# The delta layer's sixteen heads written out in a row in place of a loop over pairs of heads

## The reference, cut to what matters

```python
xn = _layernorm(x)
x = x + _L0_attn_ref(xn, ...) + _L0_ffn_ref(xn, ...)   # 16 heads; shared and routed experts
xn = _layernorm(x)
x = x + _L1_attn_ref(xn, ...) + _L1_ffn_ref(xn, ...)   # the delta layer; up, relu squared, down
```

```python
state = state * d_t
delta = (v_t - k_t @ state) * b_t
state = state + outer(k_t, delta)
o     = q_t @ state
```

## Time and profile before

| what | value |
| --- | --- |
| runs | 1971.49, 1990.26, 1990.32 us |
| profiled execution | 1971.39 us, span 1969.4 us |
| instructions counted as busy | 35372 |
| TensorE busy | 1749.0 us, 89% of the span |
| VectorE busy | 1519.3 us, 77% |
| ScalarE busy | 1226.4 us, 62% |
| GpSimd busy | 636.4 us, 32% |
| mean granted TensorE clock | 0.971 of full speed |
| data DMAs | 73.55 MB, 11.7% of 16 engines |
| instruction DMAs | 153 packets, 2.11 MB |

### The profile page before, as it was taken

How to read it: one execution, slowest core, us unless ns; L and a number is a source line. 1 busy time by engine, 2 the same in 40 slices (tenths; PEclk the granted TensorE clock), 3 DMA queues, 4 the chain that set the end, 5 groups by cost and what they waited for, 6 DMA issues and landing times.

```text
span 1969.4 us, 35372 instructions
## 1 busy us (share of the span) xinstructions
PE 1749.0 (89%) x12824; PEld 1303.0 (66%) x12824; DVE 1519.3 (77%) x2421; ACT 1226.4 (62%) x2155; POOL 636.4 (32%) x442
## 2 busy tenths in 40 slices
PE   7899999999899778889888889888988888988976
PEld 5667676767657566667766667666776666756665
DVE  8788888888674787887777878778777787877853
ACT  3253534444355567777677877768767786777862
POOL 2212222231230535336053261432605326144140
PEclk9999999999999899999999999999999999999988
DMA  3011110101032001101101011010110101101000
GB/s 131 32 62 38 54 61 31 61 31 62 3 99 65 17 16 39 33 23 33 56 23 33 23 34 55 23 34 23 33 55 23 33 23 34 55 23 33 7 1 22
DMA packets 51465, 75.66 MB, mean 38 GB/s; under 512 B 3392, under 2 KB 41792, under 8 KB 51184
## 3 DMA queue, kind: packets, MB, share of 16 engines
q1 hardware_dynamic: 51312, 73.55, 11.7%
HBM read 72.29 MB, written 1.25 MB: 37 GB/s over the span
## 4 chain that ended last, share of the span: by engine, by line
PE 39%; DVE 12%; ACT 10%; issue 9%; POOL 2%; ACTq 0%; DVEq 0%; POOLq 0%
PE bank L897 6%; PE bank L731 6%; PE bank L852 5%; PE bank L742 4%; DVE d_sil L1311 4%; PE bank L790 2%; DVE d_Rb L1377 2%; PE bank L800 2%; PE bank L764 2%; POOL d_dec L1629 2%; DVE d_W L1385 2%; PE bank L873 1%; PE bank L875 1%; PE bank L874 1%; ACT d_TT L1149 1%
## 5 line engine op out<-in xcount | busy, mean ns | idle before, releaser
L1311 DVE SCALAR_TENSOR_TENSOR d_sil<-d_pre,d_w,d_sil 128x1024 f32<-128x1024 f32 x192 | 298.1, 1553 | 5.9 <-ACT d_pre L1081 5.6
L1635 POOL TENSOR_TENSOR d_Rb<-d_V,d_ones 128x512 bf16<-128x512 f32 x32 | 48.0, 1511 | 711.0 <-ACT d_V L1110 711.0
L1363 DVE CAST_PREDICATED d_X<-tables_sb,bank 128x512 bf16<-128x512 int32 x192 | 134.3, 700 | 147.6 <-PE bank L790 146.9
L731 PE MATMUL bank<-xnT,d_w 128*128 128x512 f32 x480 | 244.1, 644 | 0.8
L189 PE MATMUL bank<-xnT,a_w 128*128 128x512 f32 x512 | 237.0, 597 | 0.0
L1145 ACT ACTIVATE d_T<-bank 128x512 bf16<-128x512 f32 x160 | 98.5, 616 | 107.4 <-PE bank L800 105.1
L1629 POOL TENSOR_TENSOR d_dec<-d_dec,d_qk 128x384 f32<-128x384 f32 x128 | 133.2, 1064 | 44.2 <-DVE d_N L1344 44.2
L852 PEld LDWEIGHTS bank<-d_W,d_N 128*128 128x128 f32 x1024 | 122.7, 193 | 35.0 <-DVE d_W L1385 22.4
L189 PEld LDWEIGHTS bank<-xnT,a_w 128*128 128x128 f32 x512 | 90.9, 192 | 78.5 <-issue 78.5
L731 PEld LDWEIGHTS bank<-xnT,d_w 128*128 128x128 f32 x480 | 89.2, 202 | 79.3 <-issue 79.3
L489 POOL TENSOR_TENSOR a_hidc<-a_hid,a_comb 128x512 f32<-128x512 f32 x32 | 44.4, 1387 | 295.0 <-DVE a_hid L336 295.0
(11 more groups left out here) (211 smaller groups left out, 4497.9 us busy)
## 6 DMA issues: line engine op xcount, KB each, us to landing
d_dec<-decay_scratch SPq DMA_DIRECT2D x32, 512.0 KB, 5.7
a_w<-w SPq DMA_DIRECT2D x16, 897.0 KB, 4.6
d_w<-w SPq DMA_DIRECT2D x16, 776.0 KB, 4.8
a_comb<-comb_scratch SPq DMA_DIRECT2D x16, 512.0 KB, 5.5
d_dec<-decay_scratch SPq DMA_DIRECT2D x32, 256.0 KB, 6.0
d_wo<-w SPq DMA_DIRECT2D x16, 256.0 KB, 3.0
f_w<-w SPq DMA_DIRECT2D x8, 256.0 KB, 3.7
tables_sb<-tables SPq DMA_DIRECT2D x1, 1056.0 KB, 8.4
```

The costliest lines, as they stand in the source:

```text
L731: last = pe.matmul(psum[bank][:, :], cols(slot, (c * KT + k) * P, P), xnT[:, k, h * HALF:(h + 1) * HALF], start=(k == 0), stop=(k == KT - 1))
L1311: dve.scalar_tensor_tensor(sil[c][:, :, :], pre[c % 2][:, :, tap:tap + S], cols(slot, OC + 4 * c + tap, 1), sil[c][:, :, :], ALU.mult, ALU ...
L1363: dve.copy_predicated(left(Xp[lv][:, v], lv), mask.unsqueeze(1).broadcast_to([P, 8, 64]).rearrange("p n (g w) -> p n g w", w=lv), psum[4 + ...
```

## The change

In `layer1_phase` the helper `loop` becomes a Python loop that calls the body for each head with integers. The order of the instructions within every engine's stream, the buffers and the semaphores' counts stay as they are. The hardware loop is gone from all five engines in this layer, with its counter, its jump, and the registers that held counts and addresses. The code of the layer becomes longer: heads 2 to 13 now stand twelve times in each stream where two heads stood before.

```diff
         def loop(engine, body, begun=0):
 
-            if not begun:
-                body(0, 0, 0)
-            body(0, 1, 1)
-            with engine.Fori(1, HEADS // 2 - 1) as j:
-                for slot in range(2):
-                    body(j, slot, j * 2 + slot)
-            body(HEADS // 2 - 1, 0, LAST - 1)
-            body(HEADS // 2 - 1, 1, LAST)
+            for i in range(begun, HEADS):
+                body(i // 2, i % 2, i)
```

## The result

The changed kernel takes 1958.04 us (median of four runs, 1953.93 to 1960.94); the kernel before, with a fourth run, 1987.11 us (1971.49 to 1990.32). The two medians alone give a ratio of 0.985; the recorded comparison of the runs gives 0.9886, with a 95% interval of 0.9845 to 0.9926: faster by 1.1%, clear of the noise and less than 2%. The forecast was 1957.4. The profiled execution took 1959.84 us with a span of 1957.8, against 1971.39 and 1969.4, so 11.6 us of span are to be accounted for; the rest of the difference of medians is the spread of the kernel before, to which the last experiments come.

What follows compares the result with a forecast made beforehand. TensorE holds 39% of the chain of waits, 9% is unexplained issue, which the change can reach. Jumps cost 20.9 us, clock dips take part back: 1971.39 - 14.0 = 1957.4 us, range 1948 to 1977.

Steps and rivals of the forecast that it cites:

- sum of heads 2 to 13: Delta layer's written-out heads: 12 x 80.42 = 965.0 us against 979.04 in the loop, 14.0 us gained.
- The jump is TensorE's: Delta layer's loop end: the stall ahead of turn_v's transposes is on TensorE, with 1.54 us of issue.
- Its price, 4.17 us: Each of five delta-layer jumps: 3.30 us in the head before it plus 0.87 in the next; 20.9 us together.
- Register work: Inside each delta-layer head: written out, it saves 0.15 us, making a clean head 79.0 us.
- The dips take part of it back: Clock falls behind TensorE's wait at invert's first level come loose, leaving 14.0 us gained of the jumps' 20.9.
- mean of four undisturbed heads, 80.42 us: Heads 1, 2, 13 and 14, with no jump before or behind, taken as the length of each written-out head.
- The longer code: Instruction fetching in the delta layer: traffic stays, no stalls, cost nothing; rival of late fetches 2007 us, chance 0.03.
- six blocks a head: Delta-layer instruction fetches: a looped head already fetches six blocks, and the number stays about six when written out.
- The median: Two runs' extra 18.9 us placed in the loop, so it goes; rival that it stays: 1976.3 us, chance 0.22.
- The tail: Heads 14, 15 and the end keep their code: nothing on the mean, 2 us in the range.
- all dips settle at the bad place: Rival: every written-out delta-layer head loses clock as head 14 does, time 1970.1 us; chance 0.09.

Runs made afterwards that it cites:

- the filling: Eight matmuls with unused results in each invert, in TensorE's wait for ScalarE: changed kernel with them 1933.71 us, kernel before with them 1950.51 us.
- before_again: The kernel before, unchanged, profiled once more to see where its slower runs spend the surplus: 1978.42 us, heads 2 to 13 sum to 985.62 us.

## Why the prediction was right

The time (1957.4 against 1958.04) and the sum of heads 2 to 13 (965.0 against 964.69) were right, by their steps too. That they are right to within a microsecond is luck: the four runs of the changed kernel lie 7 us apart, the profiled one took 1959.84, and the sum is a mean of four heads of three different lengths, times twelve. The steps:

- **The jump is TensorE's.** Right. With TensorE alone written out the gaps are gone, with all but TensorE they stay.
- **Its price, 4.17 us.** Right as a difference of those heads, but made of two parts that I had not separated: about 2 us of stall (1.9 to 2.4), and the clock's fall behind it, which makes the rest. Without the fall, as with four heads in a pass or with the filling, 1.8 to 1.9 remain.
- **Register work.** The forecast took 0.15 us a head; it is 0.2 (79.17 against 78.96), and it sits on the other engines. That registers are the reason was not tested.
- **The dips take part of it back.** Right, and this decided the size. Between the two first profiles the tails of the heads (last gated output to the next head) lose 16.1 us, and the stretch ahead of line 886, where the dips are, grows by 1.4 in spite of the registers saved and of the late starts that went with the jumps. The forecast let 20.9 + 1.8 - 14.0 = 8.7 us come back. Measured, the six odd heads fell in `invert` for 1.5 us each, about 9, and all twelve together now for 17.2, so 8 came back. That this is as much as the falls behind the jumps had cost, so that the clock's part cancels, the forecast did not say. The mean of four undisturbed heads, 80.42 us, met 80.39, with a luck that other kernels lack: written out on TensorE alone the mean is 80.96, and 80.76 without the 0.2.
- **The longer code.** Right: no gap inside a head, and fewer fetches. By "Runtime: NRT & Kernel Launch", section "Instruction fetch mechanics", of the Trainium skill, straight code is fetched ahead while a jump out of what the engine keeps must wait. The two packets at TensorE's jump, VectorE's 3.08 us in the first layer's loop of six heads, and the pure data traffic of the two-head loop agree. The 51 and 108 ns of the Trainium skill, page "Advanced Engine Details and Errata", section "Control Flow Timing", can hold at most for a jump to code at hand: in the delta layer it took 1.9 us. That the number of TensorE's own instructions decides, as I took it from 300 matmuls against 1270, is not shown: with 900 its jump showed no price. And the forecast's six blocks a head are those of queue 8 alone; queue 14 has four more in the same window.
- **The median.** The forecast read two settled values into three runs. There are none: the fourth run took 1983.96 us and the later ones lie all over the range from 1970 to 1994. I gave the loop the larger share of the 18.9 us, and before_again agrees for the 7 us that it has: the place of the dips in the pairs, not a longer stall. The idea that a pair keeps one fixed alignment was too simple: in that run some passes have an even head that falls and others do not.
- **The tail.** The 2 us that the forecast allowed for head 14, head 15 and the end were used: 1.3 less and 2.2 more. The 1.8 us ahead of the heads it had put at nothing. They are not the first layer's heads, whose time did not move, and in the twelve profiles that first matmul of line 224 starts anywhere from 39.95 to 41.91 us.

The rival that all dips settle at the bad place came nearest to true elsewhere: in the kernels with TensorE alone written out, and with four heads in a pass, half of the heads and more fell that way. Taking off the 0.2 us a head (2.4 in each) and two jumps of 1.9, that cost 4.4 us in the one (971.5 - 2.4 - 964.7) and 7.4 in the other (978.3 - 2.4 - 3.8 - 964.7) beyond the dips of the changed kernel.

## What to carry to other kernels

Find a loop's jump in the timeline of the engine that is short of time, as idle time called "issue" at the same place of each pass; with a large body, writing it out is worth the stall times the number of jumps, and with a small one perhaps nothing. Look at every engine that jumps, since a late one passes its delay on, and check each "issue" gap against the kernel's waits. Then ask what the granted clock does behind every idle stretch of TensorE: here its falls, 17 us, were worth more than the change, and eight matmuls that compute nothing useful took them away. While such falls are about, compare kernels by stretches between fixed instructions and not by total times, since any edit also moves the places where the clock falls.

## What the runs showed that was not expected

- Filling 1.7 us (71.62 - 69.94 us of TensorE's work in head 2) of a wait of 2.2 us with useless matmuls made the changed kernel 24 us faster in the median (1958.04 to 1933.71), without a longer head anywhere.
- A jump can be paid for on another engine and at another place: in the first layer's loop of six heads VectorE stood for 3.08 us at its jump, and TensorE's gap, which the profile calls "issue", came 14 us later.
- The change took away no loss to the clock in sum: 17.1 us in heads 2 to 13 before, 17.2 after.
- Much of what looked like noise of the kernel before is the place of the clock's falls: 6.6 of the 7.0 us between its two profiled executions. Whether its whole spread (23 us in thirteen runs on one chip) goes with the filling (5 us in four) is open; with both layers written out and the filling, four runs still lie 10 us apart.
